# A transformer block on one core: loops written out, combine weights as tiles loaded by DMA, one fp32 down matmul

## The reference

```python
# ffn(h), h = layernorm(x): 8 routed experts, 2 per token, 176 inner features, and a shared one
probs = softmax(h @ gate_w.T); topk_w, topk_i = top_k(probs, 2)
combine = sum(one_hot(topk_i, 8) * (topk_w / sum(topk_w))[..., None], axis=1)
g = einsum('th,ehi->eti', h, w_gate); u = einsum('th,ehi->eti', h, w_up)
eo = einsum('eti,eih->eth', silu(g) * u, w_down)
out = einsum('te,eth->th', combine, eo)
out = out + sigmoid(h @ shared_gate_w.T) * ((silu(h @ sw_gate) * (h @ sw_up)) @ sw_down)
...
x = x + 0.5 * ffn(layernorm(x))
x = x + attention(layernorm(x))      # rms-normed and rotated q, k; softmax over 2048 keys
x = x + 0.5 * ffn(layernorm(x))
```

## Time and profile before

| what | us |
|---|---|
| median of 3 runs | 2161.27 (2158.22 to 2164.5) |
| the profiled execution | 2164.42 |
| its span, first to last instruction | 2162.6 |
| mean clock granted to TensorE, share of full | 0.935 |

### The profile page before, as it was taken

One profiled execution on the slowest core, in us unless ns is written; L12 is line 12 of the kernel. 1 busy time (PEld: TensorE's weight loads), 2 busy tenths in 40 slices (PEclk: granted clock), 3 DMA queues, 4 the chain that ended last, 5 costly groups with the idle time before them and its releaser, 6 DMA issues. The chain is left out here.

```text
span 2162.6 us, 39219 instructions
## 1 busy us (share of the span) xinstructions
PE 1972.4 (91%) x11035; PEld 755.8 (35%) x11035; DVE 1670.5 (77%) x1908; ACT 1408.2 (65%) x2706; POOL 342.0 (16%) x395
## 2 busy tenths in 40 slices
PE   4799997949999999999999999999999988699998
PEld 2566665711222222222222222222222213466665
DVE  7555555659989989898989999898989933655554
ACT  2444443604888878887888888887888883344443
POOL 3245442210000000000000000000000000054544
PEclk9899997856999999999999999999999997699999
DMA  4000000220010000010010010010010000000000
GB/s 105 1 1 0 0 1 1 75 86 1 18 33 19 18 31 21 18 33 18 18 34 18 18 32 18 18 33 18 18 33 18 19 24 24 0 6 10 5 10 10
DMA packets 34624, 46.72 MB, mean 22 GB/s; under 512 B 6830, under 2 KB 25843, under 8 KB 34446
## 3 DMA queue, kind: packets, MB, share of 16 engines
q1 hardware_dynamic: 30286, 42.28, 6.2%
q10 hardware_dynamic: 4160, 2.10, 0.4%
HBM read 33.22 MB, written 10.75 MB: 20 GB/s over the span
## 5 line engine op out<-in xcount | busy, mean ns | idle before, releaser
L1253 DVE TENSOR_REDUCE at_mx<-ps 128x1 f32<-128x1024 f32 x1024 | 1206.5, 1220 | 92.6 <-PE ps L1171 77.7
L1128 ACT ACTIVATE at_prob<-ps 128x512 f32<-128x512 f32 x2048 | 1056.9, 604 | 212.7 <-PE ps L1189 202.5
L1171 PE MATMUL ps<-k_head,q_head 48*128 48x512 bf16 x2048 | 716.7, 400 | 30.6 <-PEq L766 23.7
L1189 PE MATMUL ps<-q_head,k_head 51*128 51x512 bf16 x1924 | 590.7, 388 | 52.8 <-ACT at_prob L1128 27.7
L1199 PE MATMUL ps<-at_prob,vals 128*32 128x512 f32 x4096 | 554.8, 614 | 0.2
L1189 PEld LDWEIGHTS ps<-q_head,k_head 51*128 51x128 bf16 x1924 | 144.6, 94 | 677.9 <-ACT at_prob L1128 552.0
L716 POOL TENSOR_TENSOR e_hidden_lo<-e_full,e_hidden_hi 128x512 fp32r<-128x512 f32 (+1 forms) x208 | 269.0, 1293 | 434.0 <-ACT e_hidden_hi L645 434.0
L641 ACT ACTIVATE e_silu<-ps 128x512 f32<-128x512 f32 (+1 forms) x208 | 124.1, 597 | 282.1 <-PE ps L595 282.1
L678 DVE TENSOR_TENSOR e_prod<-e_silu,ps 128x512 f32<-128x512 f32 (+1 forms) x208 | 143.0, 688 | 189.4 <-PE ps L595 173.1
L1171 PEld LDWEIGHTS ps<-k_head,q_head 48*128 48x128 bf16 x2048 | 152.5, 94 | 225.9 <-DVE at_mx L1253 197.2
L683 DVE TENSOR_TENSOR e_full<-e_prod,ps 128x512 f32<-128x512 f32 (+1 forms) x208 | 142.8, 687 | 43.5 <-DVE e_prod L678 41.7
(11 more groups left out here) (186 smaller groups left out, 1293.4 us busy)
## 6 DMA issues: line engine op xcount, KB each, us to landing
q_head<-q_rows SPq DMA_DIRECT2D x64, 96.0 KB
k_head<-k_rows SPq DMA_DIRECT2D x64, 96.0 KB
q_head<-q_rows SPq DMA_DIRECT2D x64, 64.0 KB
k_head<-k_rows SPq DMA_DIRECT2D x64, 64.0 KB
q_rows<-qk_parts SPq DMA_DIRECT2D x8, 384.0 KB, 3.2
k_rows<-qk_parts SPq DMA_DIRECT2D x8, 384.0 KB, 3.3
sum_rows<-at_sums SPq DMA_DIRECT2D x128, 18.0 KB
x<-in_L_attn_x_dram ACTq DMA_DIRECT2D x4, 512.0 KB, 7.3
```

What stands on the lines that cost most here:

```text
L1128: act.activation(prob[:, g % PROBS, c, :], ps[:, S + bank(i, g, c, last), :], ACT.Exp).then_inc(exped, 1)
L1171: one = pe.matmul(ps[:, at, :], q[i][HALF:HALF + KR, (j // CHUNKS) * P:(j // CHUNKS + 1) * P], k[i][HALF:HALF + KR, c * BLK:(c + 1) * BLK] ...
L1189: pe.matmul(ps[:, S + bank(i, g, c, last), :], k[i][0:KS, g * P:(g + 1) * P], q[i][0:KS, c * BLK:(c + 1) * BLK], start=True, stop=True).th ...
L1253: dve.tensor_reduce(mx[i][:, j // 2, j % 2:j % 2 + 1], ps[:, at:at + 2, :].rearrange("p a t -> p (a t)"), AX.X, ALU.max).then_inc(max_redu ...
```

## The change

1. All loops are written out: `for it in range(...)` takes the place of `with eng.Fori(...)` in the expert stages (all eight blocks) and in attention, on all engines. No instruction inside is changed by that in attention.
2. Routing keeps the nine combine weights in fp32: the bf16 split goes, the 32 transposes are of fp32, and `combT` has 9 rows. SP stores it in four pieces to a tensor in HBM (`comb_rows`).
3. In the expert stages SP loads, per block and chunk, a tile `cw` of 128 rows by 512 tokens in which each row is its expert's row of `comb_rows`, repeated. A chunk that two experts share takes two loads; that is 20 loads a block. A chunk's tile for the next block is loaded as soon as GpSimd has used the present one.
4. GpSimd multiplies silu by `cw`, VectorE multiplies that by up. The spread matmul, the rounding on ScalarE and the subtraction on GpSimd go. `silu`, `part` and `hidden` have two buffers each.
5. The down product is one fp32 matmul a chunk, with the weights unsplit; the split of the down weights in the first norm goes, and so does `expert_rows` with its load and cast.

```diff
@@ def over_blocks @@
-            with eng.Fori(0, NB // 2 - 1) as it:
-                for par in range(2):
-                    turn(it * 2 + par, par, False)
-            turn(NB - 2, 0, False)
-            turn(NB - 1, 1, True)
+            for blk in range(NB):
+                turn(blk, blk % 2, blk == NB - 1)
@@ expert_phase, TensorE @@
-                    pe.wait_ge(weighted, n - 1)
+                    pe.wait_ge(hidden_ready, n - 1)
...
-                pe.matmul(ps[:, SPREAD + i, :], expert_rows[:, cols], combT[:, tokens],
-                          start=True, stop=True).then_inc(spread, 1)
...
-                for m, (wp, hp) in enumerate(PASSES):
-                    last = pe.matmul(ps[:, Y, :], wdown[wp][0:rows[c], c, :], hidden[hp][0:rows[c], at, :],
-                                     start=(c == 0 and m == 0), stop=(c == CH - 1 and m == len(PASSES) - 1))
+                pe.matmul(ps[:, Y, :], wdown[0:rows[c], c, :], hidden[0:rows[c], (par + c) % 2, :],
+                          start=(c == 0), stop=(c == CH - 1)).then_inc(downed, 1)
@@ expert_phase, GpSimd @@
+            def weigh(blk, par, c):
+                n, i = blk * CH + c, (par + c) % 2
+                pool.wait_ge(silued, n + 1)
+                pool.wait_ge(cw_loaded[c], (blk + 1) * (16 * len(pieces[c])))
+                if not (isinstance(n, int) and n < 2):
+                    pool.wait_ge(hidden_ready, n - 1)
+                pool.tensor_tensor(part[0:rows[c], i, :], silu[0:rows[c], i, :], cw[0:rows[c], c, :],
+                                   ALU.mult).then_inc(weighted, 1)
@@ expert_phase, VectorE @@
+            def multiply(blk, par, c):
+                n, i = blk * CH + c, (par + c) % 2
+                dve.wait_ge(weighted, n + 1)
...
+                    dve.wait_ge(downed, n - 1)
+                dve.tensor_tensor(hidden[0:rows[c], i, :], part[0:rows[c], i, :], up, ALU.mult).then_inc(hidden_ready, 1)
@@ expert_phase, SP @@
+            def load(blk, c):
+                for a, b, expert in pieces[c]:
+                    row = comb_rows[expert:expert + 1, bass.ds(blk * BLK, BLK)]
+                    sp.dma_start(cw[a:b, c, :], row.broadcast_to([b - a, BLK])).then_inc(cw_loaded[c], 16)
+            def turn(blk, last):
+                if not last:
+                    for c in range(CH):
+                        sp.wait_ge(weighted, blk * CH + c + 1)
+                        load(blk + 1, c)
+                if out_dram is not None:
+                    sp.wait_ge(added, blk + 1 + PRIME)
...
+            sp.wait_ge(comb_stored, 16 * (NB // 2))
+            for c in range(CH):
+                load(0, c)
@@ attention_phase, TensorE (the other engines alike) @@
-            with pe.Fori(0, TURNS // BUFS) as it:
+            for it in range(0, TURNS // BUFS):
```

More of the change, by code:

```diff
@@ L437, in _, with routing_phase @@
             def _(sp):
[L438 to L441 removed]
+                for one in late:
+                    sp.wait_ge(*one)
+def routing_phase(nc, sem, tag, ps, logits, rank, ident, combT, comb_rows, comb_stored):
     step = sem(tag + "_step")
@@ L559, in expert_phase @@
     rows = [P] * (CH - 1) + [TAIL]
-    SLOTS = 4
-    fours = 2 * CH - 3 * (-2 * CH % SLOTS)
-    slot = [n % SLOTS if n < fours else (n - fours) % 3 for n in range(2 * CH)]
-    assert fours >= 0 and fours % SLOTS == 0
+    cw_loaded = [sem(f"{tag}_cw_loaded{c}") for c in range(CH)]
+    pieces = []
+    for c in range(CH):
+        cuts = [0] + [r for r in range(1, rows[c]) if (c * P + r) % I == 0] + [rows[c]]
+        pieces.append([(a, b, (c * P + a) // I) for a, b in zip(cuts, cuts[1:])])
     with ExitStack() as tmp:
@@ L631, in turn @@
                 tr.then_inc(turned, 1)
-            over_blocks(pe, first, turn)
+            over_blocks(first, turn)
         @block.scalar
@@ L707, in _ @@
             prime(dve, added)
-            over_blocks(dve, first, turn)
-        @block.gpsimd
-        def _(pool):
-            with pool.Fori(0, NB // 2) as it:
-                for n2 in range(2 * CH):
-                    pool.wait_ge(rounded, it * 2 * CH + n2 + 1)
-                    r = rows[n2 % CH]
-                    pool.tensor_tensor(hidden[LO][0:r, slot[n2], :], full[0:r, n2 % 2, :],
-                                       hidden[HI][0:r, slot[n2], :].bitcast(F32), ALU.subtract).then_inc(hidden_ready, 1)
-        if out_dram is not None:
-            @block.sync
-            def _(sp):
-                with sp.Fori(0, NB) as blk:
+            over_blocks(first, turn)
+        @block.sync
+        def _(sp):
+            def load(blk, c):
[4 more added lines that the diff above has]
+                if not last:
+                    for c in range(CH):
+                        sp.wait_ge(weighted, blk * CH + c + 1)
+                        load(blk + 1, c)
+                if out_dram is not None:
                     sp.wait_ge(added, blk + 1 + PRIME)
@@ L725, in _ @@
                                  x[:, bass.ds(blk * TPB, TPB), :]).then_inc(stored, 16)
+            sp.wait_ge(comb_stored, 16 * (NB // 2))
+            for c in range(CH):
+                load(0, c)
+            for blk in range(0, NB - 1):
+                turn(blk, False)
+            turn(NB - 1, True)
+            if out_dram is not None:
                 sp.wait_ge(stored, 16 * NB)
@@ L1076, in _ @@
                     replace(h - 1, (h - 1) % BUFS)
-            with pool.Fori(2, BH // BUFS - 1) as it:
+            for it in range(2, BH // BUFS - 1):
                 for i in range(BUFS):
@@ L1107, in _ @@
             place_maxima(0, 0)
-            with sp.Fori(0, BH // BUFS - 1) as it:
+            for it in range(0, BH // BUFS - 1):
                 for i in range(BUFS):
@@ L1272, in _ @@
                 turn(h, h)
-            with dve.Fori(1, TURNS // BUFS) as it:
+            for it in range(1, TURNS // BUFS):
                 for i in range(BUFS):
```

126 lines of the change are left out of this document (56 added, 70 removed).

## The result

The changed kernel takes 2075.84 us (median of 4 runs, 2074.65 to 2076.99); the kernel before took 2162.89 in the same comparison. The ratio is 0.9597, 95% interval 0.9581 to 0.9613: 87 us less, where 68.7 were forecast. The profiled execution took 2074.9 us, its span 2073.1. The time lies inside the range, but two large terms were off in opposite directions.

A forecast was written before the change was run, and what follows sets the result against it. TensorE's own work was taken to bound the experts, and nine loop jumps to lie on attention's path. Terms -36.9 + 12.6 - 41.4 - 2.7 - 0.3 = -68.7 gave 2095.7 us profiled, 2092.6 median; range 2070 to 2120.

The forecast's parts named there:

- Attention: Attention loops written out: the nine jumps back, 4.1 us each, gained whole, -36.9 us; -33 if part is something else.
- Everything inside stays: Attention loops: writing them out changes nothing inside a turn, so heads stay 39.01 us apart and only jumps go.
- Chunk: Expert stages on TensorE: 2.58 us a chunk becomes 1.46 + 0.93 = 2.39, gain 0.19; bounds 2.31 and 2.47.
- The six passes pay one change of operand form, as now, and keep their 1.46: Expert chunk on TensorE: the six passes ahead of the down work still take 1.46 us.
- Rival 1, pass for pass: Expert chunk: fp32 takes four passes for four, chunk stays 2.58 us; 38 us lost, 2131 us; chance 0.05.
- Rival 2: Attention: code volume, not the jump, stops TensorE, so written-out code stops as often; 36.9 us lost, 2129; chance 0.04.
- Rival 3, the lock: Expert chain: GpSimd locks VectorE out, multiplies wait for each other, 2.9 us a chunk, 2195 us; chance 0.02.
- Rival 4, late tiles: SP's queue, 20 loads a block: tiles come late; at 2 us a load, 2237 us; chance 0.04.
- The chain: Expert stages, gate through silu, GpSimd and VectorE: 3.8 us, covered by TensorE's 4.78 for two chunks.
- The starts: Start of each expert stage: slower transposes, store and first tile load; +6.3 us each, bounds +3 and +9; together +12.6.
- The ends: End of each expert stage, last gate to the sum's copy: 6.66 us becomes 4.9, -1.7 a stage.
- Weights: First normalisation: down weights no longer split, so TensorE waits less; -2.7 us, bounds 0 and -3.5.

The follow-up runs named there:

- Experiments 1 to 3: 1: changed kernel, attention loops put back, 2105.66 us; 2: changed kernel, two ScalarE waits in other order, 2046.22; 3: kernel before, only attention loops written out, 2143.56.
- experiments 4 and 5: Both from the kernel before. 4: one fp32 down matmul for three passes, 2203.25 us; 5: spread matmul left out, 2079.49 us.
- fp32_down: Kernel before with only its down matmul changed, one fp32 matmul in place of three passes; 2203.25 us, ratio 1.0189.
- experiment 9, tiles_for_block_0: Changed kernel with tiles loaded for block 0 of each expert stage only and used for all blocks; 2077.36 us, ratio 0.9606.
- experiment 6: Changed kernel with one down pass of the high parts in place of the fp32 matmul, down weights split again; 2006.06 us, ratio 0.9278.
- code_moved: Kernel before with 24 unused semaphore increments ahead of the attention loops on TensorE and on ScalarE; 2164.42 us, ratio 1.0010.
- no_spread: Kernel before with the bf16 matmul that spreads the combine weights left out; 2079.49 us, ratio 0.9609.
- loops_back: Changed kernel with attention's five loops put back as loops; 2105.66 us, ratio 0.9741.
- swap_early_tiles: Changed kernel with the two ScalarE waits in other order, plus all block 0 tile loads issued ahead of the stage barrier; 2069.66 us, ratio 0.9575.

## Why the prediction came out as it did

The time fell inside the range, and in part by luck: attention gave 22.4 us less than forecast, beyond its own bound, and the chunks 27.4 us more, beyond theirs.

**Bounds.** Right: TensorE's own work bounded the experts and still does, and the nine halts at the jump were on the path.

**Attention, -36.9 forecast, -14.5 measured: wrong, and below its own bound of -33.** The jumps' price of 36.9 was gained whole, and 29 heads of 0.71 us more, four of them 0.28 longer still, took 21.8 of it back. The step that failed is "Everything inside stays". Straight code changed the instructions inside: the wait that ScalarE is late for got an instruction of its own, 0.06 us in a cycle that TensorE and ScalarE close 16 times a head. Experiments 1 to 3 show it from three sides. The trace before had a row that said so: the written-out head 30, from 1725.95 to 1765.66, takes 39.71, and the prediction took its 39.01 from inside the loop only.

**Chunk, 2.39 forecast, 2.24 measured: the largest miss, 27 us, and outside its bounds of 2.31 to 2.47.** Two steps failed. "The six passes pay one change of operand form, as now, and keep their 1.46": they take 1.38, because the longer entry that the 1.46 held, 0.32 ahead of the spread, went with the 27-row spread and no other came in its place (experiments 4 and 5). And the fp32 matmul took 0.86, not the 0.93 of the earlier trace rows, which were read among matmuls of another kind.

**Rival 1, pass for pass**, is refuted as a time but nearly right as a mechanism. The Trainium skill, page "FP8 and Floating Point Precision", section TensorE Precision Notes, gives true fp32 four passes; the measured 0.86 is a little less, 3.8 passes of 0.2285. By passes alone the chunk went from 10 x 0.2285 = 2.29 to 2.24. The other 0.29 of the 0.34 gained were the longer entries round the spread and behind the first down pass. The prediction credited the gain to the fp32 matmul, where fp32_down shows the kernel slower by it.

**Rival 2, loops stop by volume of code**: refuted; there is no issue wait in the straight code of attention. **Rival 3, the lock**: refuted at 1271 and 688 ns. **Rival 4, late tiles**: refuted; in blocks 1 to 7 of e1 GpSimd waits for no DMA, and experiment 9 shows the blocks as long without the loads. From 150 to 240 us a load took 0.30 to 1.18 us to issue, 0.39 in the mean, and landed 1.7 to 3.3 us later; the prediction had 0.64 (its row gives 0.63) and 3.6 to 4.5.

**The chain**: right, 3.7 against 3.8 (experiment 6).

**The starts, +12.6 forecast, +8.8 measured.** The cause was right, the size within its bounds. The transposes took 5.60 against 3.60 (+2.0, taken as +2.7), TensorE's gap was 3.90 where about 5 was forecast (the first tile landed 3.7 us behind its issue, taken as 3.1), and it came back below full pace: the passes from 77.67 are 0.43 apart until about 80.

**The ends, -3.4 forecast, -3.0 measured**: right.

**Weights, -2.7 forecast, -5.3 measured: mis-sized.** The mechanism was right. Before, the third stall of VectorE left TensorE idle a second time, and its granted clock from 47 to 59 us was 0.69; after, it stayed at 1.00 to the end of the stage. The windows, before and after:

```profile
47.00:59.00 12.00, 9.25 (x44) 6.67 (x44) 4.49 (x12) 4.30 (x13) 0.51 (x1) 0.69 0.01 1
```

```profile
45.00:52.40 7.40, 6.16 (x44) 4.31 (x42) 2.50 (x8) 4.55 (x15) 0.00 (x0) 1.00 0.01 2
```

Both hold the last 44 matmuls of the stage, in 9.25 us of busy time at 0.69 and in 6.16 at 1.00. Only the stall itself was in the sum, not the return at the lower clock. The runs without the split take 28.9 to 29.8 us for the stage, those with it 34.4 to 36.5.

**The q/k stage, -6.0, not forecast.** Its code is untouched. It took 86.6 to 86.7 us in two kernels and 88.5 to 92.6 in the others, also in some whose code up to there is the changed kernel's (tiles_for_block_0: 90.4). What goes with it is the clock, in the windows of the whole stage, before and after:

```profile
368.79:461.38 92.59, 61.05 (x344) 50.77 (x345) 41.58 (x69) 42.59 (x80) 19.31 (x18) 0.72 0.25 86
```

```profile
332.37:419.01 86.64, 52.05 (x344) 43.34 (x345) 41.41 (x69) 42.01 (x80) 19.33 (x18) 0.83 0.27 92
```

The same 344 matmuls are busy 61.05 us at a granted clock of 0.72 and 52.05 at 0.83. The two kernels of 86.6 to 86.7 us have 0.83 in this stage, all others 0.72 to 0.78. Why the clock differs there was not tested. I count these 6 us to no part of the change.

So the forecast's terms, corrected: attention 22.4 too much; chunks 27.4 too little; weights, starts, load and ends 6.9 too little; and 9.0 in parts forecast at nothing. 68.7 - 22.4 + 27.4 + 6.9 + 9.0 is 89.6, the span's 89.5 but for rounding.

## What to carry to other kernels

Before writing a loop out, look at what carries each wait inside it: put the wait that is met last first in the code, so that the other gets the separate instruction, and look for a piece of the same work that is already straight to time it. Price a matmul among its neighbours, and the neighbours with it: here a small matmul of another shape cost as much in the entries beside it as in its own pass. A queue's issues ahead of a barrier counted in full, for every engine: the stage behind it began 14 us later.

## What the runs showed that I had not expected

- Two waits on one ScalarE instruction: 0.06 us for each group if the late one stands alone, 29 us of 1231 in heads 1 to 31 (experiment 2).
- A 27-row bf16 matmul between rounded passes: 0.47 us with its surroundings, for a pass of 0.23 (experiment 5). Rounded passes alone also have entries of 0.30 to 0.34 in place of 0.23, where the weights of the pass ahead were loaded no earlier than that pass started.
- The jump back of identical loops cost 4.1 us in three kernels (the one before, code_moved, no_spread) and 5.7 to 5.8 in two (loops_back, fp32_down). Open.
- The 20 loads of a block took 15.1 us to issue in a burst (15.2 in swap_early_tiles), 0.76 each, against 0.39 in the mean in the steady blocks. The first nine are about 0.47 apart; the slow ones come behind them.
- An untouched stage took 86.6 to 92.6 us in thirteen kernels; the shortest two have the highest granted clock, 0.83.
